# One turning matmul for each pair of batches, new engine orders, and plain f32 for the first pair's conditional products

## The reference, cut to what is computed

```python
# x (64, 128, 1024); cond weights (200, 128, 128); W (1024, 1024); A (8, 16, 1024); Bm (8, 1024, 16)
w = weights[itok_B_1_198]                      # one 128x128 matrix per batch
x = x + einsum('bct,bcd->bdt', x, w)           # conditional layer: mixes the 128 rows of a batch
a = itok_B_0_6                                 # one of 8 adapters per batch
H  = einsum('btd,od->bto', x, W)
xa = einsum('btd,brd->btr', x, A[a])           # 128 x 16 per batch
delta = einsum('btr,bor->bto', xa, Bm[a]) * scalings[a][:, None, None]
return x + H + delta
```

## Time and profile before

| | us |
|---|---|
| median of 3 runs | 771.11 (771.02 to 771.27) |
| profiled execution | 771.08 |
| its span (first to last instruction) | 769.2 |
| PE busy, share of the span | 761.3, 99% |
| DVE, ACT, POOL busy | 612.7, 504.3, 196.8 (80%, 66%, 26%) |

### The profile page before, as it was taken

The page is one execution under the profiler, slowest core; times in us unless marked ns, Lnnn a source line. Parts: engine busy times, 40 slices in busy tenths (PEclk is TensorE's granted clock), DMA queues, the critical chain, the costliest instruction groups (busy, mean ns, idle before and its releaser), DMA issues.

```text
span 769.2 us, 16746 instructions
## 1 busy us (share of the span) xinstructions
PE 761.3 (99%) x4432; PEld 721.5 (94%) x4432; DVE 612.7 (80%) x1386; ACT 504.3 (66%) x1173; POOL 196.8 (26%) x428
## 2 busy tenths in 40 slices
PE   8999999999999999999999999999999999999998
PEld 5667999999999999999999999999999999999997
DVE  6899977879777788777888777888777888777774
ACT  3476666676666676666676666676666676666673
POOL 5633211332311333212333211333212233212200
PEclk9999999999999999999999999999999999999999
DMA  9333334442334342334442343442343432343222
GB/s 321 138 131 144 124 121 147 125 149 90 111 128 147 125 148 86 116 127 139 134 144 80 114 140 129 143 132 84 124 137 123 150 129 84 121 143 123 89 90 83
DMA packets 47291, 98.32 MB, mean 128 GB/s; under 512 B 6438, under 2 KB 25894, under 8 KB 47270
## 3 DMA queue, kind: packets, MB, share of 16 engines
q1 hardware_dynamic: 46832, 97.68, 37.6%
q10 hardware_dynamic: 438, 0.39, 0.2%
HBM read 63.45 MB, written 34.60 MB: 127 GB/s over the span
## 4 chain that ended last, share of the span: by engine, by line
PE 90%; DVE 2%; issue 0%; ACT 0%; DVEq 0%; ACTq 0%
PE bank L1394 75%; PE o_ps L1455 4%; PE bank L1433 4%; PE o_ps L1454 4%; PE o_ps L1456 4%; DVE c_sb L904 0%; DVE z_lo L901 0%; DVE x_lo L901 0%; PE o_ps L1445 0%; PE bank L1438 0%; DVE x_raw L901 0%; DVE w_lo L901 0%; ACT z_hi L518 0%; DVE bank L904 0%; PE bank L1454 0%
## 5 line engine op out<-in xcount | busy, mean ns | idle before, releaser
L1394 PE MATMUL bank<-w_hi,x_hi 128*128 128x342 f32 (+2 forms) x1200 | 390.4, 325 | 1.1 <-ACT c_sb L518 1.1
L1394 PE MATMUL bank<-w_lo,x_hi 128*128 128x342 f32 (+2 forms) x1200 | 387.1, 323 | 0.0
L1394 PE MATMUL bank<-w_hi,x_lo 128*128 128x342 f32 (+2 forms) x1200 | 386.5, 322 | 0.0
L1394 PEld LDWEIGHTS bank<-w_hi,x_hi 128*128 128x128 f32 x1200 | 225.8, 188 | 9.7 <-ACT c_sb L518 2.2
L1394 PEld LDWEIGHTS bank<-w_lo,x_hi 128*128 128x128 f32 x1200 | 225.6, 188 | 2.8
L1394 PEld LDWEIGHTS bank<-w_hi,x_lo 128*128 128x128 f32 x1200 | 226.1, 188 | 0.0
L901 DVE TENSOR_TENSOR x_lo<-x_raw,x_hi 128x256 fp32r<-128x256 f32 (+1 forms) x270 | 145.0, 545 | 31.3 <-ACT x_hi L518 26.7
L518 ACT ACTIVATE x_hi<-x_raw 128x256 fp32r<-128x256 f32 (+1 forms) x270 | 133.8, 507 | 53.9 <-PE bank L1394 45.7
L303 POOL TENSOR_TENSOR w_lo<-a_ride,w_hi 128x160 fp32r<-128x160 f32 x30 | 15.6, 521 | 503.5 <-ACT w_hi L518 503.5
L518 ACT ACTIVATE c_sb<-bank 128x342 f32<-128x342 f32 x190 | 85.7, 452 | 41.4 <-PE bank L1394 39.0
L518 ACT ACTIVATE z_hi<-c_sb 128x340 fp32r<-128x340 f32 (+1 forms) x128 | 60.3, 490 | 53.0 <-DVE c_sb L904 53.0
(11 more groups left out here) (106 smaller groups left out, 888.1 us busy)
## 6 DMA issues: line engine op xcount, KB each, us to landing
x_raw<-xT SPq DMA_DIRECT2D x62, 512.0 KB, 4.2
out<-o_sb SPq DMA_DIRECT2D x62, 512.0 KB, 2.6
b_stack_raw<-b_split SPq DMA_DIRECT2D x128, 128.0 KB, 2.5
c_raw<-cond_w SPq DMA_DIRECT2D x64, 64.0 KB, 1.7
a_now<-lora_a SPq DMA_DIRECT2D x62, 64.0 KB, 3.2
w_lo_raw<-wB SPq DMA_DIRECT2D x7, 342.0 KB, 8.2
w_hi_raw<-wB SPq DMA_DIRECT2D x5, 342.0 KB, 5.8
out<-x_raw SPq DMA_DIRECT2D x4, 256.0 KB, 2.0
```

The costliest lines, as they stand in the source:

```text
L1394: last = nc.tensor.matmul(bank[:, lo:hi], x[:, left, c * C:(c + 1) * C], w[:, c, FIRST[o]:FIRST[o] + WIDTH[o]], start=opens and c == 0 and ...
```

## The change

1. **One turn a pair.** The two batches' ride columns, 64 each, lie side by side in one tile `xa_cols`. One matmul turns both into 128 columns of bank `alpha`. ACT copies its upper 64 rows into `g_sb[0]` and its lower 64 into `g_sb[1]`; the other halves of these tiles stay zero, set once at the start. Only the last pair keeps two turns (`turn1_alone`, `last_end`).
2. **New orders.** On PE the end of a pair is now: products 16, 1, 3, conditional product of batch 0's second half, product 19, the turn, product 6, loras 11, 10, 12, 00, product 12. Loras 01 and 02 follow product 17 of the next pair. ACT and DVE have new orders for all pairs; on DVE `sum_u12` and `begin_u` of the pair after the next are ahead of a pair's end. In the unrolled pair 2, `hi_u54` on ACT no longer stands ahead of `begin_c10` (the `c_sb` copy for which product 17's bank waits).
3. **The first pair's conditional products** are one plain f32 matmul of 512 columns each, in the place of three passes: whole c and whole z are copied to `c_whole` and `z_whole` by ACT. For this pair `rest_z`, `rest_c` and the separate copies of the blocks are gone.
4. **The beginning.** ACT's queue, not SP's, issues the two saves of B. SP loads c, waits for the saves, and does `load_b` ahead of `load_a`. POOL reads the adapters' numbers before it waits for the table of scalings, and does block b11 after the rides of b10 and b00. `b32` lands in another slot.

```diff
-            def turn0(i, j):
+            def turn(i, j):
                 after(pe, xa_ready[0], i, j, 0)
-                nc.tensor.matmul(bank_of(j, 0, "alpha")[:, H - P:H], xa_cols[0][:, :].bitcast(f32r), ident_r[:, :],
-                                 start=False, stop=True, skip_group_check=True).then_inc(turned[0], 1)
-
-            def turn1(i, j):
+                after(pe, xa_ready[1], i, j, 0)
+                nc.tensor.matmul(bank_of(j, 0, "alpha")[:, H - P:H], xa_cols[:, :].bitcast(f32r), ident_r[:, :],
+                                 start=False, stop=True, skip_group_check=True).then_inc(turned, 1)
...
             def condition(i, j, d, n, h, bank):
+                if not exists(i, j, d, 1):
+                    whole_condition(n, h, bank)
+                    return
...
+            def whole_condition(n, h, bank):
+                cols = slice(h * H, (h + 1) * H)
...
+                nc.tensor.matmul(bank[:, :], c_whole[:, n, :], z_whole[n][:, cols],
+                                 start=True, stop=True).then_inc(o_done[n][h], 1)
...
+            def end(i, j):
                 left("u3", i, j)
                 multiply("16", "pi12", i, j).then_inc(product_done["16"], 1)
+                after(pe, c02_begun, i, j, 0)
+                left("a001", i, j)
+                multiply("1", "alpha", i, j)
+                multiply("3", "alpha", i, j).then_inc(product_done["3"], 1)
                 if exists(i, j, -1):
                     condition0(i, j, -1, 1)
+                left("a02", i, j)
+                freed("12", i, j)
+                multiply("19", "pi02", i, j, True).then_inc(product_done["19"], 1)
+                turn(i, j)
+                after(pe, c02_half, i, j, 0)
+                multiply("6", "beta", i, j).then_inc(product_done["6"], 1)
+                after(pe, g_ready[1], i, j, 0)
+                after(pe, b_ready, i, j, 0)
+                lora("11", i, j, 0)
+                lora("10", i, j, 0)
+                lora("12", i, j, 0)
+                after(pe, g_ready[0], i, j, 0)
+                lora("00", i, j, 0)
+                left("a03", i, j)
+                multiply("12", "beta", i, j).then_inc(product_done["12"], 1)
...
             def turned_xa(i, j, d, n):
+                rows = slice(n * P // 2, (n + 1) * P // 2)
...
+                copy(g_sb[n][rows, :], o_ps[1][rows, 0:P] if alone else bank_of(j, d, "alpha")[rows, H - P:H])\
+                    .then_inc(g_ready[n], 1)
...
+            def save_b(part, z):
+                act.dma_start(b_split[:, part, :, :], z[:, :].bitcast(f32)).then_inc(b_saved, 16)
...
             copy(z_hi[0][:, :], b_raw[:, :]).then_inc(b_hi_ready, 1)
+            act.wait_ge(b_hi_ready, 1)
+            save_b(0, z_hi[0])
             made(act, "2")
             in_place("2")
             made(act, "0")
             in_place("0")
+            act.wait_ge(b_lo_ready, 1)
+            save_b(1, z_lo[0])
...
             load_x(0, 0, 1, 1)
-            sp.wait_ge(b_hi_ready, 1)
-            save_b(0, z_hi[0])
             sp.wait_ge(cond_landed, 16)
             load_c(0, 0, 0)
-            sp.wait_ge(b_lo_ready, 1)
-            save_b(1, z_lo[0])
             sp.wait_ge(adapter_landed, 16)
+            sp.wait_ge(b_saved, 32)
+            load_b(0, 0, 0)
             sp.wait_ge(first_scaled, 8)
             load_a(sp, 0, 0, 1)
-            sp.wait_ge(b_saved, 32)
-            load_b(0, 0, 0)
...
             pool.wait_ge(adapter_landed, 16)
+            first = [pool.value_load(adapter_sb[0:1, n:n + 1], min_val=0, max_val=NAD - 1) for n in range(2)]
             pool.wait_ge(s_tab_ready, 1)
-            pick_scalings(0, 0, 0)
+            for n in range(2):
+                nc.gpsimd.tensor_copy(s_now[:, n:n + 1], s_tab[:, bass.ds(first[n], 1)]).then_inc(s_picked, 1)
```

681 lines of the change are left out of this document (402 added, 279 removed).

## The result

| | before | after |
|---|---|---|
| median us | 771.19 (771.02 to 771.45, 4 runs) | 780.51 (778.95 to 783.83, 4 runs) |
| profiled execution, its span | 771.08, 769.2 | 779.34, 777.6 |

The ratio is 1.0126, with a 95% interval of 1.009 to 1.0162. The forecast was 768.6 in a range of 765.4 to 771.8, with a chance of 0.10 for slower. The scatter is new too: 4.9 us between the fastest and the slowest execution, 0.4 before.

A forecast was written before the change was run, and what follows sets the result against it. PE's work plus some 3.5 us of starting waits bounds the kernel. 771.08 - 3.5 - 1.2 - 0.4 - 0.9 + 0.6 = 765.7, then + 1.65 + 1.2 for late x gives 768.6 us, range 765.4 to 771.8.

The forecast's parts named there:

- Turns: Pairs 0 to 30 have one turn less on PE, 0.113 us each: -3.5 us.
- the order of the loras: Loras and conditional product reordered at a pair's end on PE, four loras together: 0 us.
- the expectation's rival C: A follow-up run's expectation: c_lo and sum c11 on DVE come late, product 17 waits, pair between 23.1 and 23.4 us.
- The end of a pair: ACT's g_sb copies for loras 11 and 00 are just in time, 0.0 to 0.1 us to spare: 0 us taken.
- Slower, 776: ACT's g_sb copies late for the loras at every pair's end, 30 x 0.25 us: 776 us; chance 0.10.
- Plain f32: Pair 0's four conditional products as plain f32 matmuls, 0.86 us per 512 columns: +0.6 us.
- POOL's start: POOL copies the scalings at least 0.9 us earlier, cutting PE's 1.4 wait and removing the 0.3 one: -1.2 us.
- B: PE's 0.4 us wait for b_stack and a small one at pair 1's turn go: -0.4 us.
- Pair 2: The hi_u54 copy no longer delays c10 on ACT; window of 24.10 against 23.15 us: -0.9 us.
- x late: Saves on ACT's queue delay pair 1's x by 4.0 us; PE waits 1.65, then +1.2; 766.7 to 770.2; chance 0.40.
- The rides late: Saves queue behind x, load_a follows load_b, product 5 of pair 1 waits 2.1 us: 767.8 us; chance 0.12.

The follow-up runs named there:

- the copies first: Changed kernel with, in the loop's ACT order, both g_sb copies moved ahead of hi_a02 and hi_of_c; median 774.29 us.
- the kernel with wide saves alone: Changed kernel with only another b_split layout, so each save of B is one transfer of 128 rows; median 780.13 us.
- The reverse exchange in the kernel before: Kernel before with load_b, and its wait for the saves, put ahead of load_a; median 771.68 us.

## Why the prediction was wrong

**Turns.** Right: 0.27 for a turn with the pass behind it, in both kernels. That the order of the loras costs nothing was right too (0.79 for the five steps with the copies first). With ACT in time a pair takes 23.10 to 23.11, 0.05 above the 23.05 named; over the loop this makes the gain 1.5 us smaller than -3.5. The traces with the copies first show where it goes. At the end of a pair, all engines:

```profile
415.38 1.34 DVE L974 TENSOR_TENSOR c_sb<-bank,c_sb 128x342 f32<-128x342 f32 x3
415.76 0.19 PEld L1525 LDWEIGHTS bank<-w_hi,x_lo 128*128 128x128 f32 x1
416.00 0.19 PEld L1525 LDWEIGHTS bank<-w_hi,x_hi 128*128 128x128 f32 x1
```

The first of the three sums is c11, 0.50 long, so it ends at 415.88. The weight load at 416.00 is that of product 17, which waits for c11 and was due at 415.76 + 0.157 = 415.92. In the pair after it the load is 0.11 late, and in both it starts 0.10 after the sum's semaphore. So this is the expectation's rival C, by the traces; no run moved the sum with the loras over 128 rows.

**The end of a pair.** The failed step, and most of the miss: "I take 0", the wait of the loras for ACT's copies. It measured 0.36 a pair, 27 x 0.36 = 9.7 of the 11.9 us between 768.6 and 780.51. With -0.11 for the turn this is +0.25 a pair. The rival "Slower, 776", with a chance of 0.10, is what happened; that it named 0.25 as well is luck, since it meant a wait of 0.25 and had it from a late c_hi or a long x part, neither of which came. The working had the path right (ACT behind product 19), and the due times too: with the copies first the weights are loaded at T + 0.90 and T + 1.38. Wrong were the lengths on ACT. `hi_a02` starts at T + 0.26 and not T + 0.20, and each of the three instructions counts with its full duration, since the copy at row 64 takes ACT's overlap away. This comes to T + 0.97 and T + 1.72 in place of T + 0.78 to 0.88 and T + 1.27 to 1.4. A slack worked out as 0.0 to 0.1 with an untried shape in its chain deserved more than a chance of 0.10, above all when it is paid 28 times.

**Plain f32.** Right to the digit: one product of 512 columns (two records in the trace) takes from 44.29 to 45.15, 0.86.

**POOL's start.** In the profiled execution PE's wait is 0.8 for 1.45, but PE, the table of scalings and the first loads each come some 0.5 later in it, and in other runs of the new order the wait is 0.8 to 1.9. Of -1.2 about -0.6 is left in this execution (the turn at 30.66 for 31.23).

**B.** The -0.4 was named "if B comes no later". It came no earlier either: `load_b` was issued at 28.64 (28.72 before) and `b_stack` was ready at 34.61 (34.43), while PE was there sooner. So the wait for it grew from 0.4 to 1.2 and took back the gain at POOL's start: product 17 of pair 1 is 0.3 later than before, and not 1.6 earlier.

**Pair 2.** Too small: -0.9 was taken, it gave -1.7. The window was read 0.7 short, and DVE was no limit in the new order. Which of the edits gave it, the place of `hi_u54` or DVE's lighter work in the plain f32 products, no run separates.

**x late.** Too large by far. Issued on ACT at 15.3 and 16.7, the saves moved their first packets only at 19.5. In 19:22 they had a quarter of the traffic. x landed 10.6 after its issue at the median of its two transfers (9.7 before), the second of them at 23.9 (22.2 before), 1.7 later and not 4.0. DVE waited 0.6 for it and began its sums 0.4 later than before, and the turn waited for nothing. The sharing itself is as the Trainium skill, "DMA: Bandwidth & Descriptors", section "Queues, rings and completion order", has it: in the kernel with wide saves alone, queue 1 and queue 10 (ACT's) split the stretch 19:23 in two.

```profile
q10 hardware_dynamic: 227, 0.86, 52.4%
q1 hardware_dynamic: 227, 0.83, 50.5%
```

What the prediction had too large is what the saves take from x: it let x wait for them for 2.7 to 5.3, and while x moved they had a quarter of the traffic (0.29 of 1.21 MB in 19:22), most of them going after it. The 4 us between issue and first packet spared x little, since x's own packets began only in 18:19, behind the blocks of W.

**The rides late.** This rival, at 0.12, also happened: 2.5 us at product 5, where its sum had 2.1. Its reason was half of the truth. A was issued at 31.7 and not 28.3, since `load_b` takes 3.1 us of SP's queue; and POOL's chain was not 6.9 us, a constant, but depends on what DVE does beside it (7.5 here). The reverse exchange in the kernel before shows it: there the rides were ready at 38.9, and nothing waited.

In sum: the likeliest case, x late, came at less than half its size and cost PE nothing, the loop was put at no wait at all, and two of the rivals came true together.

## What to carry over

Where an order leaves a chain next to no slack, and an instruction in it has a shape that no row of the trace shows, price the chain with no overlap at all, and multiply by the number of rounds before giving the case a small chance. A DMA put ahead of another in an issuing queue must be costed with its waits and its own issue time (here 3 us for a `load_b`), and the engine that uses the late one with the neighbours that it will then have. And an idle stretch of some 2 us on TensorE may cost its clock as well.

## What was not expected of the hardware

- ACT: a 64-row copy that starts at row 64 removes the 0.1 us overlap at one to three successive instructions, 0.36 us where it is three; a 64-row copy that starts at row 0 removes none.
- PE: matmuls over 64 rows among ones over 128 cost 0.6 us a pair with six of them in two groups (starts 0.24 to 0.27 apart at a change, for 0.157).
- POOL: eleven instructions take 3.3 us with DVE idle beside them and 4.4 to 10.0 beside DVE's work; DVE's busy time alone does not give the length (6.9 with 6.9 busy, 7.5 with 5.8).
- DMA: a write of 512 KB laid out as 8 groups of 16 rows kept to half of the engines (share 0.50 to 0.58, 197 to 219 GB/s); as 128 rows it shared all of them (1.02 to 1.05, 377 to 426 GB/s together with x). On ACT's queue, under a full load of SP's, the first packet came 3.6 to 4.2 us after the start of the issue (which itself took 0.4 to 1.2), when SP's blocks of W were nearly through.
- TensorE's clock: in some executions 3.4 us at half level, beginning 1.0 to 1.3 us after work resumed from a wait of 1.9 to 3.6 us; in others a wait of 2.0, 2.5 or 3.8 us had no such stretch.
